# The softmax shift of an attention unit: written into PSUM by ScalarE instead of added by matmuls

## The reference

```python
x = L0_attn_x                                  # 2048 tokens of 128
mod = (_silu(L0_c) @ L0_wmod).reshape(1, 6, 1, -1)
h = _layernorm(x) * (1 + ca) + sa
# 16 heads of 64; 2048 positions attend to 2048 positions in each
scores = softmax(einsum('bhid,bhjd->bhij', xq, xk) * 64 ** -0.5)
out = einsum('bhij,bhjd->bhid', scores, xv)
x = x + ga * einsum('bso,ho->bsh', out, wo)
h = _layernorm(x) * (1 + cb) + sb
x = x + gb * ffn(h)                            # 8 experts, the best 2 of a token, and a shared one
```

## Time and profile before

| | us |
|---|---|
| median of 3 runs | 1363.32 (1362.63 to 1363.95) |
| profiled execution, its time | 1362.54 |
| its span in the profile | 1360.7 |
| PE busy in the span | 1338.5 (98%) |
| POOL busy in the span | 1188.5 (87%) |
| DVE, ACT busy | 918.3, 669.5 |
| mean granted TensorE clock | 0.995 of full speed |

### The profile page before, as it was taken

One profiled execution on the slowest core, in us unless ns is written; L12 is line 12 of the kernel. 1 busy time (PEld: TensorE's weight loads), 2 busy tenths in 40 slices (PEclk: granted clock), 3 DMA queues, 4 the chain that ended last, 5 costly groups with the idle time before them and its releaser, 6 DMA issues.

```text
span 1360.7 us, 21599 instructions
## 1 busy us (share of the span) xinstructions
PE 1338.5 (98%) x8714; PEld 699.9 (51%) x8714; DVE 918.3 (67%) x1024; ACT 669.5 (49%) x837; POOL 1188.5 (87%) x537
## 2 busy tenths in 40 slices
PE   7999999999999999999999999999999999999998
PEld 5544545454554545454544545454545545454565
DVE  5767667676767676676766676676767676746755
ACT  6454545454544545454544545554545545465331
POOL 2499999999999999999999999999999999999443
PEclk8999999999999999999999999999999999999999
DMA  7010202020010202020100102020201002003231
GB/s 203 3 45 1 47 2 47 1 47 1 22 27 1 47 1 48 1 47 1 44 4 9 39 1 48 1 48 1 47 1 27 22 1 48 1 1 63 63 99 57
DMA packets 31957, 41.51 MB, mean 31 GB/s; under 512 B 4298, under 2 KB 15186, under 8 KB 31858
## 3 DMA queue, kind: packets, MB, share of 16 engines
q1 hardware_dynamic: 31714, 40.13, 12.4%
q10 hardware_dynamic: 144, 0.00, 0.0%
HBM read 13.70 MB, written 1.11 MB: 11 GB/s over the span
## 4 chain that ended last, share of the span: by engine, by line
PE 95%; DVE 3%; ACT 1%; DMA 0%; issue 0%; SPq 0%; DVEq 0%
PE ps L1200 35%; PE ps L1123 15%; PE ps L1176 9%; PE ps L1179 9%; PE ps L1182 9%; PE ps L1100 4%; PE ps L1226 2%; PE ps L1104 2%; PE ps L442 2%; PE ps L428 2%; PE ps L1213 2%; PE ps L443 2%; DVE peak_parts L930 1%; PE ps L1188 1%; DVE ps L950 0%; DMA probs<-in_L_attn_wq_dram 0%
## 5 line engine op out<-in xcount | busy, mean ns | idle before, releaser
L857 POOL TENSOR_TENSOR acc<-acc,probs 128x1024 f32<-128x1024 f32 x448 | 1068.3, 2385 | 68.2 <-ACT probs L791 3.4
L930 DVE TENSOR_REDUCE peak_parts<-ps 128x2 f32<-128x1024 f32 x512 | 624.1, 1221 | 304.7 <-PE ps L1123 299.9
L791 ACT ACTIVATE probs<-ps 128x1024 f32<-128x1024 f32 x512 | 496.8, 1023 | 398.3 <-PE ps L1182 322.6
L1200 PE MATMUL ps<-probs,v_sb 128*64 128x512 f32 x2048 | 507.5, 606 | 0.0
L1200 PEld LDWEIGHTS ps<-probs,v_sb 128*64 128x64 f32 x2048 | 126.3, 136 | 195.9 <-issue 166.5
L1176 PE MATMUL ps<-q_hi,d_swap_hi 64*128 64x512 f32 x512 | 201.5, 394 | 0.0
L1176 PE MATMUL ps<-q_hi,d_hi 64*128 64x512 f32 x512 | 201.4, 393 | 0.0
L1179 PE MATMUL ps<-q_lo,d_hi 64*128 64x512 f32 x512 | 200.3, 391 | 0.0
L1182 PE MATMUL ps<-q_hi,d_swap_lo 64*128 64x512 f32 x512 | 200.2, 391 | 0.0
L1182 PE MATMUL ps<-q_hi,d_lo 64*128 64x512 f32 x512 | 200.1, 391 | 0.0
L1179 PE MATMUL ps<-q_lo,d_swap_hi 64*128 64x512 f32 x512 | 200.0, 391 | 0.0
(11 more groups left out here) (147 smaller groups left out, 1084.4 us busy)
## 6 DMA issues: line engine op xcount, KB each, us to landing
k_swap_hi<-k_hi SPq DMA_DIRECT2D x64, 128.0 KB, 2.3
d_swap_hi<-d_hi SPq DMA_DIRECT2D x64, 128.0 KB, 2.3
d_swap_lo<-d_lo SPq DMA_DIRECT2D x64, 128.0 KB, 2.3
token_weights<-weights_dram SPq DMA_DIRECT2D x32, 256.0 KB, 3.2
probs<-in_L_ffn_w_dram SPq DMA_DIRECT2D x2, 512.0 KB, 5.5
shifts<-shift_sb SPq DMA_DIRECT2D x64, 2.0 KB
out_dram<-probs SPq DMA_DIRECT2D x4, 256.0 KB, 3.0
x_in<-in_L_attn_x_dram SPq DMA_DIRECT2D x1, 960.0 KB, 8.8
```

Source lines behind the costliest of these rows:

```text
L791: act.activation(probs[:, kt % PROBS, :], ps[:, 2 * place:2 * place + 2, :].rearrange("p a b -> p (a b)"), ACT.Exp, scale=SCALE).then_inc( ...
L857: pool.tensor_tensor(total, total if kt > 1 else probs[:, 0, :], probs[:, kt % PROBS, :], ALU.add).then_inc(added, 1)
L930: dve.tensor_reduce(peak_parts[:, :, i // STRETCHES, i % STRETCHES], ps[:, bank:bank + 2, :], AX.X, ALU.max).then_inc(peak_free, 1)
L1200: mm = pe.matmul(ps[at:at + HEAD_DIM, PV_BANK, :], v_sb[:, p, chunk_of(kt) * HEAD_DIM:(chunk_of(kt) + 1) * HEAD_DIM], probs[:, kt % PROBS, ...
```

## The change

ScalarE now writes the negated maxima into the four score banks before a unit begins (`fill`), and all the score matmuls add to what is there. Before the body four matmuls write the banks once (`opened`). The maxima get onto all partitions by two DMAs in a row: `shift_sb` goes to DRAM (`shift_dram`, 4 KB), and from there a second one reads the same 4 KB into each of the 128 partitions (`shift_wide`, 512 KB in all). SP waits for the first between them. `fill` stands behind the exponential of tile 15 on ScalarE, and `scores` of tiles 0 and 1 wait for it. Beside that three tables change: `shift` moves from place 26 to 22 in both halves, `out` from 23 to 30, the second `v` from 27 to 30, and `EARLY_PAIRS` becomes 6, which puts pair 15 at place 19 instead of 23 and two more pairs into the prologue.

```diff
-EARLY_PAIRS = 4
+EARLY_PAIRS = 6
 LONG_JOBS = (
-    {3: ("q", 0), 6: ("sum", 0), 15: ("k", 0), 19: ("k", 1), 23: ("out", 0), 26: ("shift", 0)},
-    {3: ("q", 1), 7: ("v", 0), 10: ("sum", 0), 26: ("shift", 0), 27: ("v", 1)},
+    {3: ("q", 0), 6: ("sum", 0), 15: ("k", 0), 19: ("k", 1), 22: ("shift", 0), 30: ("out", 0)},
+    {3: ("q", 1), 7: ("v", 0), 10: ("sum", 0), 22: ("shift", 0), 30: ("v", 1)},
 )
...
-            def send_shift(job, target_half):
+            def send_shift(job, target_unit, target_half):
 
                 sp.wait_ge(job_free, job.full)
-                for odd in (0, 1):
-                    sp.dma_start(
-                        shifts[odd * HEAD_DIM:odd * HEAD_DIM + 1, target_half, :].bitcast(F32),
-                        shift_sb[4 * odd:4 * odd + 4, target_half, :].bitcast(F32),
-                    ).then_inc(shift_ready, 16)
+                if not (isinstance(target_unit, int) and target_unit == 0):
+                    sp.wait_ge(shift_ready, target_unit * 16)
+                sp.dma_start(shift_dram[target_half], shift_sb[:, target_half, :]).then_inc(shift_out, 16)
+                sp.wait_ge(shift_out, target_unit * 16 + 16)
+                if not (isinstance(target_unit, int) and target_unit == 0):
+
+                    sp.wait_ge(filled, target_unit * 2)
+                sp.dma_start(shift_wide[:, :], shift_dram[target_half:target_half + 1].rearrange(
+                    "a r c -> a (r c)").broadcast_to([P, HALF])).then_inc(shift_ready, 16)
...
+            def fill(kt, target_unit):
+
+                if isinstance(target_unit, int) and target_unit == 0:
+                    act.wait_ge(opened, 1)
+                else:
+
+                    act.wait_ge(exped, target_unit * TILES + (kt - 1))
+                act.wait_ge(shift_ready, target_unit * 16 + 16)
+                act.activation(ps[:, 2 * kt:2 * kt + 2, :].rearrange("p a b -> p (a b)"), shift_wide[:, :],
+                               ACT.Copy, scale=-1.0).then_inc(filled, 1)
...
+                                if kt == TILES - 1 and not (last_head and half == 1):
+                                    for later in (0, 1):
+                                        fill(later, unit + 1)
...
-                first = isinstance(unit, int) and unit == 0
-                if not (first and kt < 2):
+                if kt < 2:
+
+                    pe.wait_ge(filled, unit * 2 + (kt + 1))
+                else:
                     pe.wait_ge(exped, unit * TILES + (kt - 1))
...
-                if kt < 2:
-                    if kt == 0:
-                        pe.wait_ge(shift_ready, unit * 32 + 32)
-                    for b in range(2):
-                        mm = pe.matmul(ps[:, slot + b, :], minus[at[b], :], shifts[at[b], half, :],
-                                       start=False, stop=True, tile_position=(b * HEAD_DIM, 0), skip_group_check=True)
...
+            for n in range(4):
+                at = slice(n % 2 * HEAD_DIM, (n % 2 + 1) * HEAD_DIM)
+                mm = pe.matmul(ps[:, n, :], k_hi[at, 0, 0:P], q_hi[at, 0, 0:BANK], start=True, stop=True,
+                               tile_position=(n % 2 * HEAD_DIM, 0))
+            mm.then_inc(opened, 1)
```

More of the change, by code:

```diff
@@ L135, in build @@
         k_raw = sb("k_raw", [P, P + HALF])
-        shifts = sb("shifts", [P, 2, BANK], F32R)
-        minus = sb("minus", [P, P], F32R)
-        minus_col = sb("minus_col", [P, 1])
+        shift_wide = sb("shift_wide", [P, HALF])
         v_sb = sb("v_sb", [P, 2, CHUNKS * HEAD_DIM])
@@ L161, in build @@
         peak = sb("peak", [P, HEAD_DIM])
-        shift_sb = sb("shift_sb", [8, 2, P], F32R)
+        shift_sb = sb("shift_sb", [8, 2, P])
         gateT = sb("gateT", [P, EXPERTS])
@@ L202, in build @@
         peak_ready = sem("peak_ready")
-        shift_ready = sem("shift_ready")
+        shift_out, shift_ready, opened, filled = sem("shift_out"), sem("shift_ready"), sem("opened"), sem("filled")
         scored, exped, pv_done, o_copied = sem("scored"), sem("exped"), sem("pv_done"), sem("o_copied")
@@ L375, in build @@
         weights_dram = nc.dram_tensor("weights_dram", [EXPERTS, TOKENS], F32, kind="Internal").ap()
+        shift_dram = nc.dram_tensor("shift_dram", [2, 8, P], F32, kind="Internal").ap()
         weights_ready = sem("weights_ready")
@@ L650, in _ @@
                 swap_d(i + 1, Job(1 + i), i, 0)
-            sp.wait_ge(shifts_zero, 1)
-            send_shift(Job(PROLOGUE_JOBS - 1), 0)
+            send_shift(Job(PROLOGUE_JOBS - 1), 0, 0)
             def body(t):
@@ L664, in body @@
                                 if kind == "shift":
-                                    send_shift(Job(jobs_at(t) + local), 1 - half)
+                                    send_shift(Job(jobs_at(t) + local), unit + 1, 1 - half)
                                 local += kind in COUNTED
@@ L698, in _ @@
                 keep_setup(n)
[L700 to L704, removed]
             act.activation(k_raw[:, 0:P], ones[:, :], ACT.Copy, scale=0.0)
-            act.activation(shifts[:, :, :].rearrange("p a b -> p (a b)"), ones[:, 0:1].broadcast_to([P, 2 * BANK]),
-                           ACT.Copy, scale=0.0).then_inc(shifts_zero, 1)
             for n in range(2, len(FIRST_SETUP)):
@@ L770, in _ @@
                 jobs += kind in COUNTED
+            for kt in (0, 1):
+                fill(kt, 0)
             def body(t):
@@ L1176, in scores @@
                     pe.matmul(ps[:, slot + b, :], hi[b][at[b], p, cols], q_hi[at[b], p, q],
-                              start=kt < 2, stop=False, tile_position=(b * HEAD_DIM, 0), skip_group_check=True)
+                              start=False, stop=False, tile_position=(b * HEAD_DIM, 0), skip_group_check=True)
                 for b in range(2):
@@ L1182, in scores @@
                     mm = pe.matmul(ps[:, slot + b, :], lo[b][at[b], p, cols], q_hi[at[b], p, q],
-                                   start=False, stop=kt >= 2, tile_position=(b * HEAD_DIM, 0), skip_group_check=True)
-                if kt < 2:
-                    if kt == 0:
-                        pe.wait_ge(shift_ready, unit * 32 + 32)
-                    for b in range(2):
-                        mm = pe.matmul(ps[:, slot + b, :], minus[at[b], :], shifts[at[b], half, :],
-                                       start=False, stop=True, tile_position=(b * HEAD_DIM, 0), skip_group_check=True)
+                                   start=False, stop=True, tile_position=(b * HEAD_DIM, 0), skip_group_check=True)
                 mm.then_inc(scored, 1)
```

5 lines of the change are left out of this document (2 added, 3 removed).

## The result

The changed kernel takes 1373.29 us (median of 5 runs, 1370.13 to 1374.93) against 1363.32 for the kernel before (1362.63 to 1365.17): a ratio of 1.0067, 95% interval [1.0056, 1.0079]. It is slower by some 10 us.

The account below looks back on a forecast made before the run. It took PE as the bound, with GpSimd (POOL) at the same pace hardly 2 us away. Terms 5.3 - 14.3 + 14.5 - 0.8 = +4.7 on 1362.54 gave 1367.2, predicted as 1368.0 us; range 1363.8 to 1373.5.

Parts of the forecast that it names:

- The upper end: Top of the predicted range, whole kernel: main case with stalls of 1.25 us (+4.2) and a slow start (+1.5), 1373.5 us.
- the lower end: Bottom of the predicted range, whole kernel: rival (a) with a quick read at the start, 1363.8 us.
- rival (a): In the body: stall at the transpose much smaller, PE then runs into GpSimd's additions; +0.8, 1364.1 us; 20%.
- the start's own lower bound: Before the first unit: 2.8 us added, with 3.2 us for the wide read and full clock.
- The start, +5.3: Before the first unit: two DMAs, first fill and low clock delay tiles 0 and 1, 5.3 us added.
- The removed pairs, -14.3: Tiles 0 and 1 of 31 units: dropping two L1188 pairs saves 0.46 us per unit, 14.3 us in all.
- The stall, +14.5: Even units, transpose behind the first weigh: PE waits for d_lo to free the bank, 0.97 us 15 times, 14.5 us.
- The end, -0.8 for the two pairs: Last units: EARLY_PAIRS 6 leaves 2 pairs fewer at 0.4 us each, 0.8 us saved.
- Rival (c): Around the stalls: PE's granted clock falls to half, losing 1.7 us 15 times, 25 us; 1393 us; 5%.
- (b): In the body: no stall, PE keeps the whole saving, -9.8, 1353.5 us; 3%.
- 75.5 to 75.6 us for two units: Sign in the body: two units take this time as before; 74.6 would be (b).
- Rival (d): At the fills: wide copy lands later than the cover allows; 1 us beyond costs 31 us, 1399 us; 5%.

Follow-up runs that it names:

- e2_tables: The kernel before with only the change's tables (shift at 22, out and v at 30, 6 early pairs), maxima still by matmuls: 1377.03 us, ratio 1.0097.
- e7_before_half_adds_no_shift_mm: The kernel before with GpSimd adding only 512 of 1024 columns, and without the L1188 matmuls in units 1 to 31: 1352.04 us, ratio 0.9921.
- e3_fill_old_tables: The changed kernel with the old tables (shift at 26, out at 23, v at 27, 4 early pairs): 1388.25 us, ratio 1.0182.
- e5_after_half_adds: The changed kernel with GpSimd adding only 512 of the 1024 columns: 1369.10 us, ratio 1.0049.
- e8_out23: The changed kernel with the even units' out back at place 23 and their shift at 24: 1366.79 us, ratio 1.0024.
- e9h_hybrid: The changed kernel with e8_out23's tables, odd units' shift also at 24, five early pairs, unit 0's maxima by L1188: 1364.45 us, ratio 1.0006.
- e4_shift23_half_adds: e1_shift23 with GpSimd adding only 512 of the 1024 columns: 1367.71 us, ratio 1.0029.
- e1_shift23: The changed kernel with the even units' shift at place 23, behind both weigh, instead of 22: 1371.98 us, ratio 1.0065.
- e11_before_relief: The kernel before with the first of a unit's 15 additions moved from GpSimd to VectorE at place 2: 1382.10 us, ratio 1.0139.
- e10_best: e9h_hybrid with the first of a unit's 15 additions moved from GpSimd to VectorE at place 2: 1382.05 us, ratio 1.0137.

## Why the prediction held, and where it didn't

The direction, the mechanism and the place were right: the stall at the transpose eats the saving, and the start is paid on top. The sum came out at +4.7 where the profiled execution shows +8.5: of its four terms the saving was much too large and the end had the wrong sign, while the start and the stall were somewhat too high and hid a part of that. That the measured time still lies in the range is luck in part. The upper end was made of stalls of 1.25 us and a slow start, and neither came. Its terms add up to 1373.7 and not to 1373.5, and the lower end takes only 0.3 us off rival (a) for a quick read, where the start's own lower bound takes 2.5; neither slip changes the forecast.

- **The start, +5.3: measured +3.75** by the first exponential, +3.3 by GpSimd's first addition. The wide read took 3.5 us (median of all 3.6), not 4.4, and DRAM's write 1.2 to the next issue, not 1.5. "The two extra pairs and the four `opened` matmuls lie in the wait for the DMAs" was wrong for this kernel: it was the DMAs that lay in the wait for the pairs, e2_tables has 2.3 us of delay without them. The Trainium skill's figures in the prediction, 5.2 us for the two DMAs, are given by "DMA: Bandwidth & Descriptors", Anatomy of one DMA, for DMAs that GpSimd issues; here SP issues them, and the two took 1.2 + 3.5 = 4.7. The low clock was granted for 10.2 us where it had been 3.4; I had allowed 0.4 us for it, and how much of the 3.75 it took isn't measured by itself.
- **The removed pairs, -14.3: measured -8.9.** Units 0 to 30 came out at +3.46; less the stalls below that is -9.6. Some 0.7 of it belongs to the two pairs fewer, which are unit 30's: it got 0.92 shorter, where an odd unit got 0.26 shorter. Without any fill, e7_before_half_adds_no_shift_mm gives 9.2 by the medians. This is the step that failed: "its price on PE is the distance to the next pair, 0.23 us", twice a unit. The first L1188 is worth it. Behind the second stands a pair that has to wait for a reduction on VectorE, so only about 0.03 to 0.05 of it is won. The chain at the unit's turn is 0.54 us from the pair to its reduction, 1.23 for this and 0.05 to the next pair, 1.82 in all (543.40 to 545.22), and PE can't go below that. I had looked at what the removed work cost and not at what it covered.
- **The stall, +14.5: measured 15 times 0.87, +13.1.** Right in place, count and cause. The 0.2 us for the reduction of `peak` is there: `step_k` to the end of `d_lo` is 2.03 us before and after, but `d_lo` now ends 532.15 - 530.47 = 1.68 us behind the start of place 22's `weigh`, where it was 526.84 - 525.38 = 1.46. Too high was the weight load: the transpose starts 0.05 us after `d_lo` ends, and I had taken 0.20.
- **The end, -0.8 for the two pairs: measured +1.27.** The two pairs are missing in unit 30, about -0.7 there, and no pair stands behind it. From unit 31 on the clock's fall to 1.2 GHz took 2.8 us, and I had no term for it; the 1.5 us that came back are one L1188 pair and something that isn't traced. Rival (c) had looked for such a fall at the stalls, and there the clock stayed at full: its 25 us didn't come. It came once in e3_fill_old_tables: PE idled 1.7 us for a fill and was busy for 1.66 of the 3.40 us up to 818.8, and in the next 3.40 the granted clock was 0.50.
- **Rival (a), GpSimd binds once the stall is small:** not reached by the changed kernel (e5_after_half_adds), but e8_out23, with the stall gone, reaches it from unit 11 on. It was the next wall, as the rows of GpSimd had it. (b) fell with the stall, and with the stall gone e9h_hybrid wasn't faster than the kernel before either. As a sign I had named 75.5 to 75.6 us for two units; they took 75.88.
- **Rival (d), the wide copy too late:** not in the changed kernel, since the read was quicker than taken, but it is the whole of e3_fill_old_tables. There PE lost over 20 us.

The last 1.4 us between 1368.0 and 1373.29 are that the profiled execution of the changed kernel lies 2.2 below its median, where I carried over 0.8 from the kernel before. Its runs spread over 4.8 us, those of the kernel before over 2.5. Falls of the clock don't make the difference: its mean was 0.990 in the two shortest of the five runs and 0.991 to 0.992 in the three longest. With GpSimd's additions halved the spread is smaller, 3.1 in e5_after_half_adds and 2.2 in e4_shift23_half_adds (e1_shift23: 5.1). What it is that makes some executions longer stays open.

More of the saving might be had with the reduction behind tile 1 out of the way, by a pair moved from place 1, for example. That was not run.

## What to carry to other kernels

Price a removed instruction by what stands behind it, not by its own length: look for the engine that its time covered (here one VectorE reduction between two pairs) and take the saving only down to that chain. When a job moves, ask who owned the shared buffer before it, and keep long work between the two: putting an output product of 1.9 us back in its place was worth 6.5 us (e8_out23 against the changed kernel). And run the halves of a change apart: here the tables cost 13.7 us, and what they were moved for gave back 3.7.

## What the runs showed of the hardware

- A VectorE addition of two SBUF tiles of 128x1024 takes 1.21 us while GpSimd is idle, and up to 3.3 us in the body, where it waits for the GpSimd addition that is running. The 32 additions of e11_before_relief on VectorE (ns, min, median, max), then the GpSimd addition that came second at unit 20 of e10_best, 0.08 us after VectorE's had begun:

```profile
L999 DVE TENSOR_TENSOR acc<-probs x32: 1214/2206/3194, 52.8 to 1239.1; 128x1024 f32<-128x1024 f32 x32
```

```profile
814.37 3.39 POOL L887 TENSOR_TENSOR acc<-acc,probs 128x1024 f32<-128x1024 f32 x1
```

  In both kernels each of VectorE's additions takes 1.21 us plus what the running GpSimd addition still had to go, less 0.13, within 0.02; and the GpSimd addition that comes second takes 1.0 us more than its 2.39. The Trainium skill, "SBUF — State Buffer", Who interferes with whom, has the port pair that the two share as an exclusive lock. The trace agrees in that the addition that comes second is the one that takes longer, by about what the first still had to go.
- VectorE's reductions from PSUM don't feel the GpSimd additions beside them: in the changed kernel the 512 take 1.22 us each on average and 1.23 at most.
- A read of 4 KB of DRAM into all 128 partitions, 512 KB in all, takes 3.3 to 4.0 us to land, median 3.6, by the issues of the changed kernel; its write to DRAM and the wait for it cost 1.2 us at the least and 1.8 at the median before the read goes out.
- The granted clock fell to 1.2 GHz, for 6.8 us, at a place where the profile shows PE busy without a gap, at the end of 24 matmuls of eight columns (3.24 us), in the changed kernel and not in the kernel before.
